# Router weights padded to 128 columns, and an accumulator cleared by ScalarE: a two-layer graph network with mixtures of experts on one Trainium2 core

## The chip, the cores and the metric

The kernel runs on one core of one Trainium2 chip. The metric is the device time of one execution in microseconds (us), taken as the median of several runs. The core has five engines that run their own instruction streams and meet only at semaphores: TensorE (PE in the profile, with its weight loads as PEld), VectorE (DVE), ScalarE (ACT), GpSimd (POOL) and SyncE (SP), which here issues most of the DMAs.

## The reference, cut to what matters

Four layers run one after the other on 6250 rows of 256 numbers and 100,000 edges sorted by destination. Everything is fp32.

```
x = x + graph_attention(layernorm(x), edges)      # 8 heads of 32
x = x + gated_ffn(layernorm(x))                   # shared MLP + 4 experts, top 2 of a softmax gate
x = x + mean_aggregate(layernorm(x), edges)       # then batch norm, relu
x = x + top1_ffn(layernorm(x))                    # 32 experts
```

The two layers that the change touches:

```
# graph attention, for every edge (s, d)
e   = leaky_relu(eh[s] + ee + et[d])
a   = exp(e - max over d) / sum over d
rst[d] = sum over the edges of d of  a * ft[s]

# gated feed-forward
gates = softmax(x @ gW + gb)          # gW is 256 x 4
top2  -> softmax of the two values -> weights of the experts' outputs
```

## The kernel before, in words

The program is a chain of stages with a barrier between them. `front` computes projected rows `ft_rows`, scores and index tables. `attend` does the softmax over edges and the weighted sums. `rank_rows` writes the sums to DRAM. `gated_experts` is the first feed-forward layer. `sum_segments`, `rank_rows`, `mean_route` and `expert_tiles` are the second half; the change does not touch them.

**attend.** The edges are laid out as 784 tiles of 128 edges, in 49 chunks of 16 tiles. For each tile GpSimd issues one indirect DMA (line 978) that gathers 128 rows of `ft_rows` into slot `c % 5` of the chunk ring `G` (`GX`, `G3`, `G4`). Four chunks are gathered already in `front` (line 511). From the sixth chunk on (`c >= GS`, number 5 counted from zero) GpSimd waits at every fourth tile until TensorE has multiplied the same tiles of the chunk that held the slot before (line 977). Per chunk, VectorE adds the scores (line 1169, `SCT`, which waits for the chunk's gathers), runs the softmax, builds one-hot matrices `AHOT` (lines 1180 and 1181) and weights the gathered rows (line 1281). TensorE multiplies rows by one-hots (line 1132). ScalarE writes the products into the accumulator `ACC` (lines 1059 and 1037), 128 partitions by 12,760 columns, at the rank of each destination. It runs two exponentials per chunk for VectorE (lines 1020 and 1024). The work on chunk 0 before its first product is `first` on each engine: VectorE's `scores`, `maxima`, `onehots`, `sums` and so on, and ScalarE's `penalties`, `exponentials`, `chain`.

`ACC` has to be zero where no edge writes. GpSimd clears it with one memset (line 961) just before its first gather of the stage, chunk 4's, and ScalarE waits for `acc_zero` before its first write (line 1042).

SyncE loads the score parts of each chunk (line 989). After the last of these it loads the feed-forward weights (line 995), the router's `GW` among them. When chunks 45, 46 and 47 have been multiplied, it reloads `x` into `GX`, piece by piece (line 1004).

**gated_experts.** The 6250 rows are 50 tiles of 125; a group is two tiles, so there are 25 groups. Written out by hand, group g on TensorE is: hidden layers of the shared MLP and the four experts (line 1906), transpose of the gate weights (line 1893, waits for VectorE's `gate_rows`), transpose of the next group's rows (line 1874), second layers (lines 1906 and 1913), spreading of the gate weights and biases (lines 1935 and 1940), then the next group's router logits (line 1885), then output layers (lines 1947 and 1952). The logits are four matmuls (2 tiles x 2 halves of the 256 features): the transposed rows `fxT` are the stationary operand, 125 columns, and `GW`, 4 columns wide, is streamed. The profile shows each fp32 matmul of this kind as two records, so eight records per group. VectorE waits for the last of them (line 1705) and then runs `gates`, a chain of small operations, later `normed` and `weigh`, which end in `gate_rows` (line 1736).

Of the kernel before, what the change touches and what calls it, by code (L numbers as in the profile page):

```python
# [22 lines left out]
ACT = mybir.ActivationFunctionType  # L23
AX = mybir.AxisListType

P = 125
N, E, D = 6250, 100000, 256
# [15 lines left out]
UT = 16  # L43
# [801 lines left out]
def attend(nc, sb, ps, sem, sems, pace, FT, PRED, CONTU, WHOLE, GX, g_in, ident, iota, SRCT, RELT, GOES, BASEI, ACC,  # L845
# [14 lines left out]
    with ExitStack() as s:  # L860
# [51 lines left out]
        sel, sel2 = sem("sel_set"), sem("sel_T")  # L912
        set_ready = sem("attend_set")
        pre_in = sems("pre_in", SL)
        pre_free, acc_zero = sem("pre_free"), sem("acc_zeroed")
        e_ready, u_ready, v_ready, x_ready = sem("scores_T"), sem("scores_U"), sem("scores_less_max"), sem("scores_exp")
        pen_ready, q_ready, qs_ready = sem("pen_ready"), sem("ends_ready"), sem("ends_by_head")
        xa_ready, xe_ready, s_ready, su_ready = sem("chain_args"), sem("chain_exp"), sem("shares_ready"), sem("shares_before")
# [14 lines left out]
        with nc.Block() as block:  # L933
            @block.gpsimd
            def _(pool):
                for one in (HSEL, HSELT):
                    nc.gpsimd.memset(one[:, :], 1.0).then_inc(sel, 1)
                nc.gpsimd.memset(FSEL[:, :, :], 1.0).then_inc(sel, 1)
                pool.wait_ge(sel, 3)
                n = 3  # L940

                for one, pat, base, mul in ((HSEL, [[-UT, H0]], 0, 1), (HSEL, [[UT, H0]], UT - 1, -1),
                                            (HSELT, [[1, 128]], 0, -UT), (HSELT, [[-1, 128]], UT - 1, UT)):
                    nc.gpsimd.affine_select(out=one[:, :], in_=one[:, :], compare_op=ALU.is_ge, fill=0.0,
                                            base=base, pattern=pat, channel_multiplier=mul).then_inc(sel, 1)
                    n += 1
                    pool.wait_ge(sel, n)

                for sign, base in ((1, 0), (-1, HD - 1)):
                    nc.gpsimd.affine_select(out=FSEL[:, :, :], in_=FSEL[:, :, :], compare_op=ALU.is_ge, fill=0.0, base=base,  # L950
                                            pattern=[[128 * sign, KD], [sign, 128]], channel_multiplier=-HD * sign).then_inc(sel, 1)
                    n += 1
                    pool.wait_ge(sel, n)

                nc.gpsimd.iota(BU[:, :], pattern=[[-1, UT]], base=0, channel_multiplier=1,
                               allow_small_or_imprecise_dtypes=True).then_inc(sel2, 1)

                for t in range(GF * UT, ES):
                    c, m = divmod(t, UT)
                    if t == GF * UT:  # L960
                        nc.gpsimd.memset(ACC[:, :], 0.0).then_inc(acc_zero, 1)
                    if t == GS * UT:
                        PADT, SEL = FFN["PADT"], FFN["SEL"]
                        nc.gpsimd.memset(PADT[:, 0:PW - 1], 0.0)
                        nc.gpsimd.memset(PADT[:, PW - 1:PW], float(SKIP)).then_inc(fw_set, 1)
                        pool.wait_ge(fw_set, 1)
                        nc.gpsimd.memset(SEL[:, :, :], 1.0).then_inc(fw_pad, 1)
                        pool.wait_ge(fw_pad, 1)

                        nc.gpsimd.affine_select(out=SEL[:, :, :], in_=SEL[:, :, :], compare_op=ALU.is_ge, fill=0.0, base=0,  # L970
                                                pattern=[[128, SEL.shape[1]], [1, 128]], channel_multiplier=-EH2).then_inc(fw_pad, 1)
                        pool.wait_ge(fw_pad, 2)
                        nc.gpsimd.affine_select(out=SEL[:, :, :], in_=SEL[:, :, :], compare_op=ALU.is_ge, fill=0.0, base=EH2 - 1,
                                                pattern=[[-128, SEL.shape[1]], [-1, 128]], channel_multiplier=EH2)
                    if m % WB == 0 and c >= GS:

                        pool.wait_ge(prod[NBK - 1], (c - GS) * CPB + m // NBK + 1)
                    pool.indirect_dma_start(G[c % GS][:, m, :], None, FT[:, :],  # L978
                                            bass.IndirectOffsetOnAxis(ap=SRCT[:, t:t + 1], axis=0)
                                            ).then_inc(g_in[c % GS], 16)  # L980

            @block.sync
            def _(sp):
# [7 lines left out]
                sp.sem_inc(pre_free, SL)  # L991
                unrolled(NCH, SL, lambda c, k, i: None, load)

                for to, of in weights:
                    sp.dma_start(to, of, allow_slow_non_contiguous=True).then_inc(fw_in, 16)
                x, X, xm_in, bias, BI, bi_in = more
# [11 lines left out]
            def _(act):  # L1008
# [13 lines left out]
                def chain(c):  # L1022
                    act.wait_ge(xa_ready, c + 1)
                    nc.scalar.activation(XA[:, :, :], XA[:, :, :], ACT.Exp).then_inc(xe_ready, 1)

                def first(c, k, i):
                    act.sem_inc(fc_ready[1], 1)
                    for step in (penalties, exponentials, chain):
                        step(c)
                    penalties(c + 1)  # L1030

                def finish(h, n):
# [5 lines left out]

                def rest(c, k, i, more):
                    steps = {3: exponentials, 9: chain}  # L1040
                    if c == 0:
                        act.wait_ge(acc_zero, 1)
                    for h in range(2):
                        act.load(regs[h], BASEI[0:1, ds(c * UT + h * HT, HT)])
                        for j in range(HT):
# [470 lines left out]
def ffn_buffers(sb, s):  # L1516

    NB = NG * EH2 // 128
    shapes = {"S1": [128, KD, SH1], "S2": [128, KD, SH2], "S3": [128, D], "E1": [128, KD, NG, EH1], "E2": [128, NG, EH2],
              "E3": [128, NB, D], "OB3": [WROW + NG + 1, D], "GW": [128, KD, NG], "GBB": [P, NG], "B1": [128, KD], "B2": [128, 1],  # L1520
              "C1": [128, NG], "C2": [128, NB], "SEL": [NG, NB, 128], "PADT": [128, PW], "BI": [P, D]}
    return {n: sb(s, f"ffn_{n}", shape) for n, shape in shapes.items()}


def ffn_weights(F, sW1, sb1, sW2, sb2, sW3, sb3, eW1, eb1, eW2, eb2, eW3, eb3, gW, gb):
# [4 lines left out]
        (F["S3"][:, :], sW3[:, :]),  # L1530
        (F["OB3"][WROW:WROW + NG, :], eb3[:, :]),
        (F["OB3"][WROW + NG:WROW + NG + 1, :], sb3.rearrange("(o n) -> o n", o=1)),
        (F["GW"][:, :, :], gW.rearrange("(k p) n -> p k n", p=128)), (F["GBB"][:, :], gb.partition_broadcast(P)),
        (F["B1"][:, :], sb1.rearrange("(k p) -> p k", p=128)), (F["B2"][:, :], sb2.rearrange("(p o) -> p o", o=1)),
        (F["C1"][:, :], eb1.rearrange("e p -> p e")),
    ]
# [12 lines left out]
def gated_experts(nc, sb, ps, sem, sems, RSUMD, RANKI, XND, F, x_in, bi_in, X, ST, MEAN, RSTD, ident, ones, epsc, SORTD):  # L1549
# [7 lines left out]
    with ExitStack() as s:  # L1557
# [49 lines left out]
        with nc.Block() as block:  # L1607
# [19 lines left out]
            def _(dve):  # L1627
# [74 lines left out]
                def gates(g):  # L1702

                    dve.wait_ge(l_ready, g + 1)
                    nc.vector.tensor_tensor(g_["l"][:, :, :], pG[0:P, 0:GT * NG].rearrange("p (k e) -> p k e", e=NG),
                                            GBB[:, :].unsqueeze(1).to_broadcast([P, GT, NG]), ALU.add).then_inc(l_read, 1)
                    dve.drain()
                    nc.vector.tensor_reduce(r_["mx"][:, :], g_["l"][:, :, :], AX.X, ALU.max)
# [152 lines left out]
            def _(pe):  # L1861
# [16 lines left out]
                def logits(g, k):  # L1878
                    pe.wait_ge(x_ready, g + 1)

                    pe.wait_ge(wt_copied, g + 1)
                    for m in range(GT):
                        o = pG[0:P, m * NG:(m + 1) * NG]
                        for c in range(KD):
                            last = nc.tensor.matmul(o, xT[k][:, c, m * P:(m + 1) * P], GW[:, c, :], start=(c == 0),
                                                    stop=(c == KD - 1))
                    last.then_inc(l_ready, 1)
# [672 lines left out]
```

## Time and profile before

| | us |
|---|---|
| median of 3 runs | 3366.17 (3363.21 to 3370.33) |
| the profiled execution's own time | 3367.67 |
| its span on the core | 3365.8 |
| attend (405 to 1372 of the span) | 967 |
| rank_rows and the start of the gated layer (1372 to 1434) | 62 |
| gated_experts from its first logits (1434 to 1872) | 438 |
| second half (1872 to the end) | 1494 |

The span is what the profiler saw between the first and the last instruction; the execution's own time is 1.9 us longer. Over the whole span TensorE is busy 74%, VectorE 57%, GpSimd 54% and ScalarE 38% of the time, but these shares mix stages with different limits. What a change is worth is read from the stage in which it lies.

### The profile page before, as it was taken

The numbers are of one execution on the slowest core, as the hardware profiler recorded it, in microseconds if no ns is written. First come the engines' busy times: TensorE is split into PE (matmuls) and PEld (weight loads), VectorE is DVE, ScalarE is ACT, GpSimd is POOL, SyncE is SP. The second block draws the span as 40 slices with busy tenths as digits, with TensorE's granted clock in tenths as the row PEclk, the third lists the DMA queues.
The fourth block names the chain that finished last, engine by engine and source line by source line (L and its number), as shares of the span: only waits on it lengthen the run. The fifth ranks groups of instructions, "written<-read, shape, count | busy, mean of one in ns | idle before, by whom it ended". The sixth has DMA issues, their size and how long they took to land. (4 is left out here: it accounts for less than half of the span.)

```text
span 3365.8 us, 49930 instructions
## 1 busy us (share of the span) xinstructions
PE 2499.3 (74%) x12770; PEld 2079.5 (62%) x12770; DVE 1930.4 (57%) x6044; ACT 1278.5 (38%) x4608; POOL 1811.0 (54%) x1886
## 2 busy tenths in 40 slices
PE   5997767666666666478878688788888888657078
PEld 5886656666665555356666566666666666546067
DVE  7971388888888887467555433333333333366245
ACT  2331145555554544432333333333333333354023
POOL 0007777777777776121000477777777777250545
PEclk9986688888878877678899656665655565755589
DMA  7345644444444446530000233333333333310443
GB/s 206 95 120 131 193 110 112 111 112 111 112 111 112 112 112 153 185 104 24 25 25 1 89 106 106 105 105 105 105 106 106 106 105 105 113 55 7 112 140 88
DMA packets 263656, 348.46 MB, mean 104 GB/s; under 512 B 153546, under 2 KB 193600, under 8 KB 262120
## 3 DMA queue, kind: packets, MB, share of 16 engines
q0 software_dynamic: 87936, 235.05, 24.9%
q1 hardware_dynamic: 175446, 110.32, 12.8%
q8 instruction: 104, 1.70, 0.2%
q14 instruction: 170, 1.38, 0.1%
HBM read 288.25 MB, written 61.20 MB: 104 GB/s over the span
## 5 line engine op out<-in xcount | busy, mean ns | idle before, releaser
L1379 POOL DMA_INDIRECT Gb<-normed_rows,SRCT x784 | 743.3, 948 | 566.4 <-SPq L1371 327.7
L1400 PE MATMUL pAb<-HOTb,Gb 128*128 128x128 f32 x3136 | 839.9, 424 | 155.3 <-DMA Gb<-normed_rows,SRCT 125.8
L1400 PEld LDWEIGHTS pAb<-HOTb,Gb 128*128 128x128 f32 x3136 | 658.1, 296 | 337.5 <-DMA Gb<-normed_rows,SRCT 279.6
L1440 DVE TENSOR_TENSOR ACC<-ACC,pAb 128x256 f32 x784 | 330.6, 422 | 644.1 <-PE pAb L1400 571.4
L978 POOL DMA_INDIRECT GX<-ft_rows,SRCT x432 | 414.2, 959 | 131.5 <-issue 130.3
L1059 ACT ACTIVATE ACC<-apA 128x254 f32 x784 | 301.0, 384 | 424.1 <-PE apA L1132 349.6
L1132 PE MATMUL apA<-AHOT,GX 128*128 128x129 f32 x1920 | 306.9, 330 | 84.7 <-DVE GX L1281 84.5
L1132 PEld LDWEIGHTS apA<-AHOT,GX 128*128 128x128 f32 x1920 | 292.1, 242 | 103.1 <-DVE GX L1281 102.6
L1419 ACT ACTIVATE HOTb<-OFFb 128x1024 f32<-128x1024 f32 x98 | 103.6, 1057 | 606.5 <-PE pAb L1400 606.4
L978 POOL DMA_INDIRECT G<-ft_rows,SRCT x288 | 275.5, 957 | 87.6 <-issue 86.0
L1415 ACT ACTIVATE OFFb<-iota,NRELb 128x128 f32<-128x128 f32 x784 | 239.6, 388 | 7.5 <-issue 1.0
L1132 PE MATMUL apA<-AHOT,G 128*128 128x129 f32 x1216 | 190.9, 326 | 53.8 <-DVE G L1281 51.5
L1132 PEld LDWEIGHTS apA<-AHOT,G 128*128 128x128 f32 x1216 | 181.2, 238 | 65.9 <-DVE G L1281 62.8
L1601 POOL DMA_INDIRECT Y<-sums_by_rank,RANKI x50 | 48.5, 970 | 179.3 <-DVE GX L1648 85.4
L1281 DVE TENSOR_TENSOR GX<-GX,apV 128x1024 f32<-128x1024 f32 x120 | 143.1, 1192 | 0.0
L533 PEld LDWEIGHTS pS<-VB,eT 128*128 128x128 f32 x784 | 116.6, 236 | 33.3 <-ACT eT L624 31.4
L1060 ACT ACTIVATE FL<-apA 128x4 f32<-128x4 f32 x784 | 134.5, 172 | 0.0
L533 PE MATMUL pS<-VB,eT 128*128 128x16 f32 x784 | 120.9, 299 | 16.9 <-ACT eT L624 12.3
L497 POOL DMA_INDIRECT C<-et_rows,DXI x1 | 2.3, 2272 | 234.9 <-DMA et_rows<-ETS 234.9
L2166 POOL DMA_INDIRECT rows_by_expert<-PAY,POSI x50 | 49.7, 995 | 140.3 <-DVE POSI L2357 125.3
L1181 DVE TENSOR_TENSOR AHOT<-apL,RELT 128x1024 f32<-128x1024 f32 x98 | 122.5, 1250 | 0.0
L2418 POOL DMA_INDIRECT out_dram<-sO,sID x80 | 77.9, 973 | 74.9 <-issue 42.0
(381 smaller groups left out, 4453.7 us busy)
## 6 DMA issues: line engine op xcount, KB each, us to landing
ebuf<-in_edge_attr_dram SPq DMA_DIRECT2D x49, 448.0 KB
Gb<-normed_rows,SRCT POOLq DMA_INDIRECT x784, 2.8
rows_by_expert<-ffn_PADT SPq DMA_DIRECT2D x1, 10360.0 KB
sT<-rows_by_expert SPq DMA_DIRECT2D x80, 129.5 KB, 2.2
GX<-ft_rows,SRCT POOLq DMA_INDIRECT x480
sums_by_rank<-rrowa SPq DMA_DIRECT2D x49, 128.0 KB, 1.7
sums_by_rank<-rrowb SPq DMA_DIRECT2D x49, 128.0 KB, 1.7
GX<-in_x_dram SPq DMA_DIRECT2D x11, 560.0 KB
```

The source lines that it names most:

```text
L533: last = nc.tensor.matmul(pS[:, m * 2 * H0:(m + 1) * 2 * H0], eT[c % 2][:, m * EP:(m + 1) * EP], VB[:, :], start=True, stop=True)
L978: pool.indirect_dma_start(G[c % GS][:, m, :], None, FT[:, :], bass.IndirectOffsetOnAxis(ap=SRCT[:, t:t + 1], axis=0)).then_inc(g_in[c % GS ...
L1059: nc.scalar.activation(acc[:, :, ds(r + 1, EP - 1)], sums[:, :, 1:EP], ACT.Copy)
L1060: nc.scalar.activation(FL[:, :, f:n + 1:n - f], sums[:, :, 0:HW:EP], ACT.Copy).then_inc(pfree[b], 1)
L1132: last = nc.tensor.matmul(pA[b][:, f * HW:(f + 1) * HW], G[c % GS][:, m, f * 128:(f + 1) * 128], HOT[c % 2][:, m, :], start=True, stop=True)
L1181: nc.vector.tensor_tensor(HOT[c % 2][:, h * HT:(h + 1) * HT, 0:EP], pL[0:EP, 256:256 + EP].unsqueeze(1).to_broadcast([EP, HT, EP]), RELT[: ...
L1281: nc.vector.tensor_tensor(v, v, pV[0:EP, 0:128].rearrange("p (h m) -> p h m", m=UT)[:, :, m:m + WB].rearrange("p h m -> p m h").unsqueeze( ...
L1379: pool.indirect_dma_start(G[g % R][m][:, :], None, TABLE[:, :], bass.IndirectOffsetOnAxis(ap=SRCT[:, t:t + 1], axis=0)).then_inc(g_in[g % ...
L1400: last = nc.tensor.matmul(pA[b][:, o:o + EP], G[k][m][:, c * 128:(c + 1) * 128], HOT[k % 2][:, m, :], start=True, stop=True)
L1415: nc.scalar.activation(OFF[k2][:, m, :], iota[0:EP, 0:EP], ACT.Abs, bias=NREL[k2][:, m:m + 1])
L1419: nc.scalar.activation(HOT[k2][:, :, :], OFF[k2][:, :, :], ACT.Relu, bias=1.0, scale=-1.0).then_inc(hot[k2], 1)
L1440: last = nc.vector.tensor_tensor(acc[:, :, ds(b, EP)], acc[:, :, ds(b, EP)], pA[q][:, o:o + KD * EP].rearrange("p (c r) -> p c r", c=KD), ...
```

## The change

1. GpSimd no longer clears `ACC`. The semaphore `acc_zero` and ScalarE's wait for it are gone. ScalarE clears `ACC` itself, in two halves of 6,380 columns: an activation Copy of a broadcast constant column with scale 0. The first half stands between `penalties(0)` and `exponentials(0)`, the second between `exponentials(0)` and `chain(0)`.
2. The router's weight tile `GW` grows from 4 to 128 columns per half (1 KB per partition). GpSimd zeroes it before chunk 5's gathers, and SyncE waits for that before it loads the weights; the load fills columns 0 to 3.
3. The four logit matmuls of a group stream 128 columns in place of 4. They write 256 columns of the bank in place of 8, and VectorE reads 4 of each 128.

```diff
@@ attend, GpSimd
                 for t in range(GF * UT, ES):
                     c, m = divmod(t, UT)
-                    if t == GF * UT:
-                        nc.gpsimd.memset(ACC[:, :], 0.0).then_inc(acc_zero, 1)
                     if t == GS * UT:
-                        PADT, SEL = FFN["PADT"], FFN["SEL"]
+                        PADT, SEL, GW = FFN["PADT"], FFN["SEL"], FFN["GW"]
+                        nc.gpsimd.memset(GW[:, :, :], 0.0).then_inc(fw_set, 1)
                         nc.gpsimd.memset(PADT[:, 0:PW - 1], 0.0)
                         nc.gpsimd.memset(PADT[:, PW - 1:PW], float(SKIP)).then_inc(fw_set, 1)
-                        pool.wait_ge(fw_set, 1)
+                        pool.wait_ge(fw_set, 2)
@@ attend, SyncE
                 unrolled(NCH, SL, lambda c, k, i: None, load)
+                sp.wait_ge(fw_set, 2)
                 for to, of in weights:
@@ attend, ScalarE
+                def clear(h):
+                    half = KD * NR // 2
+                    nc.scalar.activation(ACC[:, h * half:(h + 1) * half], iota[:, 0:1].to_broadcast([128, half]), ACT.Copy,
+                                         scale=0.0)
+
                 def first(c, k, i):
                     act.sem_inc(fc_ready[1], 1)
-                    for step in (penalties, exponentials, chain):
-                        step(c)
+                    penalties(c)
+                    clear(0)
+                    exponentials(c)
+                    clear(1)
+                    chain(c)
                     penalties(c + 1)
@@
                 def rest(c, k, i, more):
                     steps = {3: exponentials, 9: chain}
-                    if c == 0:
-                        act.wait_ge(acc_zero, 1)
@@ ffn_buffers, ffn_weights
-"GW": [128, KD, NG]
+"GW": [128, KD, 128]
-        (F["GW"][:, :, :], gW.rearrange("(k p) n -> p k n", p=128)), (F["GBB"][:, :], gb.partition_broadcast(P)),
+        (F["GW"][:, :, 0:NG], gW.rearrange("(k p) n -> p k n", p=128)), (F["GBB"][:, :], gb.partition_broadcast(P)),
@@ gated_experts, VectorE
-                    nc.vector.tensor_tensor(g_["l"][:, :, :], pG[0:P, 0:GT * NG].rearrange("p (k e) -> p k e", e=NG),
+                    nc.vector.tensor_tensor(g_["l"][:, :, :], pG[0:P, 0:GT * 128].rearrange("p (k e) -> p k e", e=128)[:, :, 0:NG],
@@ gated_experts, TensorE
-                        o = pG[0:P, m * NG:(m + 1) * NG]
+                        o = pG[0:P, m * 128:(m + 1) * 128]
                         for c in range(KD):
                             last = nc.tensor.matmul(o, xT[k][:, c, m * P:(m + 1) * P], GW[:, c, :], start=(c == 0),
                                                     stop=(c == KD - 1))
```

## Rows read from the trace of the kernel before

**Rows 1.** Busy time by stage: stretch, its length, each engine's busy us, clock, DMA.
```profile
core 0: us, PE busy (x) PEld busy (x) DVE busy (x) ACT busy (x) POOL busy (x), PEclk, DMA share, GB/s
405.00:1372.00 967.00, 637.06 (x3822) 573.42 (x3822) 814.46 (x2816) 489.84 (x2549) 704.28 (x736) 0.81 0.47 114
...
1434.00:1872.00 438.00, 353.85 (x1736) 277.09 (x1737) 264.70 (x1237) 142.16 (x317) 34.27 (x35) 0.87 0.12 36
```

**Rows 2.** Instruction groups of GpSimd in attend: busy us, mean ns, idle before.
```profile
L978 POOL DMA_INDIRECT GX<-ft_rows,SRCT x432 | 414.2, 959 | 131.5 <-issue 130.3 <-PE apA L1132 1.2
...
L961 POOL MEMSET ACC<- 128x12760 f32 x1 | 10.7, 10732 | 0.0
...
L964 POOL MEMSET ffn_PADT<- 128x258 f32 x1 | 0.3, 333 | 0.0
```

**Rows 3.** Timeline of VectorE: start us, us; the score step of chunks 1, 29, 46, 47.
```profile
427.31 0.37 DVE L1169 TENSOR_TENSOR SCT<-GX,PRE 128x128 f32<-128x128 f32 x1
...
948.80 0.36 DVE L1169 TENSOR_TENSOR SCT<-G,PRE 128x128 f32<-128x128 f32 x1
...
1290.74 0.37 DVE L1169 TENSOR_TENSOR SCT<-GX,PRE 128x128 f32<-128x128 f32 x1 [2.08 <-DMA GX<-ft_rows,SRCT]
...
1318.75 0.37 DVE L1169 TENSOR_TENSOR SCT<-GX,PRE 128x128 f32<-128x128 f32 x1 [9.54 <-DMA GX<-ft_rows,SRCT]
```

**Rows 4.** Timeline of the stage's start, ScalarE and GpSimd.
```profile
406.56 1.28 ACT L1020 ACT_TABLE_LOAD   x1
...
407.90 10.73 POOL L961 MEMSET ACC<- 128x12760 f32 x1
...
422.51 0.24 ACT L1024 ACTIVATE XA<-XA 8x48 f32<-8x48 f32 x1 [8.85 <-DVE XA L1235]
...
433.64 0.38 ACT L1059 ACTIVATE ACC<-apA 128x254 f32 x1 [0.15 <-issue]
...
440.50 0.95 POOL L978 DMA_INDIRECT GX<-ft_rows,SRCT  x1 [0.16 <-issue]
```

**Rows 5.** VectorE's copy into the one-hots: ns min/median/max, first and last start.
```profile
L1180 DVE COPY AHOT<-GOES x49: 169/175/5093, 413.6 to 1342.2; 128x16 f32<-128x16 f32 x49
```

**Rows 6.** Instruction groups of ScalarE, kept apart by shape.
```profile
L1419 ACT ACTIVATE HOTb<-OFFb 128x1024 f32<-128x1024 f32 x98 | 103.6, 1057 | 606.5 <-PE pAb L1400 606.4
...
L1014 ACT ACTIVATE CTU<-CONTU 128x129 f32<-128x129 bf16 x49 | 15.3, 312 | 11.1 <-DVEq L1153 5.6
```

**Rows 7.** Timeline of SyncE's queue near the end of attend: the first reloads of x.
```profile
1306.42 1.63 SPq L1004 DMA_DIRECT2D GX<-in_x_dram  x4
```

**Rows 8.** Waits in 1434 to 1872: us in total, times, longest.
```profile
DVE gate_l L1705 <- PE fpG L1885: 12.9, 25, 3.7
```

**Rows 9.** Timeline of gated_experts: VectorE's first gate step in four groups, logits of the last.
```profile
1647.43 0.17 DVE L1705 TENSOR_TENSOR gate_l<-fpG,ffn_GBB 125x8 f32<-125x8 f32 x1 [0.32 <-PE fpG L1885]
...
1661.78 0.17 DVE L1705 TENSOR_TENSOR gate_l<-fpG,ffn_GBB 125x8 f32<-125x8 f32 x1 [0.31 <-PE fpG L1885]
...
1802.58 0.17 DVE L1705 TENSOR_TENSOR gate_l<-fpG,ffn_GBB 125x8 f32<-125x8 f32 x1 [0.31 <-PE fpG L1885]
...
1815.50 1.03 PE L1885 MATMUL fpG<-ffn_GW,fxT 128*125 128x4 f32 x8
...
1816.58 0.17 DVE L1705 TENSOR_TENSOR gate_l<-fpG,ffn_GBB 125x8 f32<-125x8 f32 x1 [0.31 <-PE fpG L1885]
```

**Rows 10.** TensorE records: one's ns min/median/max, then two merged runs of records.
```profile
L1885 PE MATMUL fpG<-ffn_GW,fxT x200: 250/250/373, 1433.4 to 1850.7; 128*125 128x4 f32 x100
...
478.24 2.05 PE L1132 MATMUL apA<-AHOT,GX 128*128 128x129 f32 x16 [1.13 <-DVE GX L1281]
...
1653.30 3.54 PE L1906 MATMUL fpM<-fxT,ffn_E 128*128 128x250 f32 x16
```

**Rows 11.** TensorE's busy time and granted clock (third number; 1.00 is 2.4 GHz).
```profile
1644.10:1647.50 3.40, 3.40 (x27) 1.00 0.00 0
1647.50:1650.90 3.40, 3.40 (x9) 0.51 0.02 5
```

More of the change, by code:

```diff
@@ L914, in attend @@
         pre_in = sems("pre_in", SL)
-        pre_free, acc_zero = sem("pre_free"), sem("acc_zeroed")
+        pre_free = sem("pre_free")
         e_ready, u_ready, v_ready, x_ready = sem("scores_T"), sem("scores_U"), sem("scores_less_max"), sem("scores_exp")
@@ L1519, in ffn_buffers @@
     shapes = {"S1": [128, KD, SH1], "S2": [128, KD, SH2], "S3": [128, D], "E1": [128, KD, NG, EH1], "E2": [128, NG, EH2],
-              "E3": [128, NB, D], "OB3": [WROW + NG + 1, D], "GW": [128, KD, NG], "GBB": [P, NG], "B1": [128, KD], "B2": [128, 1],
+              "E3": [128, NB, D], "OB3": [WROW + NG + 1, D], "GW": [128, KD, 128], "GBB": [P, NG], "B1": [128, KD], "B2": [128, 1],
               "C1": [128, NG], "C2": [128, NB], "SEL": [NG, NB, 128], "PADT": [128, PW], "BI": [P, D]}
```

## The prediction

> **What bounds the kernel now.** I read the busy time by stage first. In attend no engine is full: VectorE is busy 814 of 967 us and GpSimd 704 [rows 1]. So the next view is what each of the two waits for. GpSimd's gathers cost 0.96 us each and have 0.3 us of issue time in front (131.5 us over 432), 1.25 us together; of their idle time only 1.2 us was spent waiting for a free slot [rows 2], and the 288 gathers of the other slots look the same. GpSimd runs flat out through the stage. Sixteen gathers make 20.1 us per chunk.
>
> The timeline of VectorE's score step shows who is late. From chunk 1 to chunk 29 it starts every (948.80 - 427.31)/28 = 18.6 us and waits for nothing. By chunk 46 it waits 2.08 us for gathered rows [rows 3]; all of the 17 chunks from 30 to 46 wait so and come about 20.1 us apart. VectorE uses up the lead of four chunks, and after chunk 29 the gather stream alone sets the time. A microsecond taken from GpSimd before its last gather is a microsecond off the stage, provided VectorE and the slots allow it.
>
> In the gated layer TensorE is busy 354 of 438 us [rows 1], but it is not alone on the path. VectorE's first gate step waits for the logits in all 25 groups [rows 8], and the loop logits, gates, gate weights, transposes, second layers, logits closes: 14.00 us from one gate step to the next, whose logits started 1.08 us before it [rows 9]. What is added to the end of the logits is added to each group.
>
> **The change part by part.**
>
> *The memset.* It held GpSimd 10.73 us from 407.90, directly ahead of chunk 4's gathers [rows 2, 4]. They start that much earlier: -10.7 us. `GW` is zeroed in the same stream, 256 columns; the memset of 258 columns took 0.33 us [rows 2]: +0.3. SyncE's new wait is for that memset, done at about 430; the weight loads behind it come after the last score-part load, hundreds of microseconds later, and are as many as before: nothing.
>
> *VectorE in the prologue.* One of the 49 copies of line 1180 took 5.09 us against a median of 0.175, the one at 413.6 that ran beside the memset; it ended with it [rows 4, 5]. Two steps behind it were stretched as well. Without the memset chunk 0's chain moves up by about 3.5 us: 4.9 for the copy, less 1.3 of one-hot and scan work that ran meanwhile. The Trainium skill, "SBUF — State Buffer", section "Who interferes with whom", says that VectorE and GpSimd share a port pair as an exclusive lock, so the later one blocks fully, and that ScalarE has ports of its own. The trace agrees with the first half (5.09 us). The page would have the new clearing disturb nobody; no row shows it.
>
> *ScalarE's clearing.* 1024 columns take 1.057 us and 129 take 0.312, so 0.83 ns per column and 0.2 fixed [rows 6]; a half of 6,380 columns takes 5.5 us. If all of it went at 1.057/1024 it would be 6.6. Chunk 0: the table load at 406.56 [rows 4] marks the end of the penalties; first half to 412.1, table load of 1.28 to 413.3. The first exponential feeds the work behind the copy of 413.6 [rows 5], so it is about on time. Second half 413.7 to 419.2; the next exponential, at 422.51 before [rows 4], would be wanted 3.5 earlier, at 419.0. It comes 0.2 late, and VectorE has the second half of the one-hots to do in between. So the clearing hides behind VectorE's prologue. With 6.6 us halves VectorE is 0.9 us late; cover gone entirely, each half would cost up to 6.6. ScalarE's own order puts the clearing ahead of the products, the fourth of which reached it at 433.64 [rows 4].
>
> *The slot wait.* Chunk 5's first gather was at 440.50; now it wants to go at 440.5 - 10.7 + 0.3 = 430.1. It needs four tiles of chunk 0 multiplied, which was so just before 433.6 [rows 4] and, 3.5 earlier, at 430.0. So this wait goes from nothing to 0 to 0.6 us; I take 0.2. If VectorE gained nothing it would be 3.4. After that TensorE moves at 18.6 per chunk and GpSimd at 20.1, so the slots open up. Does VectorE still fall behind the gathers before the end? It starts 10.2 - 3.5 = 6.7 us behind the shifted stream and gains 1.5 per chunk: five chunks later than 30. Chunk 35 is well before 48. Attend: -10.7 + 0.3 + 0.2 = -10.2; bounds -10.6 and -7.0.
>
> *The end of attend.* The reload of x starts when chunk 45 is multiplied, at 1306.4, and chunk 47's rows come 9.54 us late beside it [rows 3, 7]. Both sides of that collision move with the gathers, so it stays as it is.
>
> *The logits.* Before, eight records in 1.03 us, one of them 0.25 [rows 9, 10]: (1.03 - 0.25)/7 = 0.111 us apart, though only 4 columns are streamed. So the weight load of 125 columns sets the pace. Streaming 250 columns, 16 records take 3.54: about 0.21 apart, so 128 columns need 0.108, which fits under 0.111. The run with 129 columns and 128 weights has 16 in 2.05, about 0.118 apart [rows 10]. The pace is hardly changed; what is added is the tail of the last record, between nothing (its bound by the load) and 124 of 250 columns of 0.21, 0.10. Per group: low 0.02, high 7 x 0.007 + 0.10 = 0.15. I take 0.08, times 24 loops: +1.9 us; bounds 0.5 and 3.6. VectorE's strided read is of 8 elements still: nothing. The Trainium skill, "TensorE: Matmul & The Clock Gate", section "Back-to-back issue gap", speaks against the widening: a warm matmul of 64 columns or fewer takes about 60 cycles and one of 128 takes 134. Those 74 cycles at 2.4 GHz are 31 ns; times 8 and 24 it is an estimate of 5.9 us and would make the sum -5.3. The pace of 0.111 at 4 columns says that the floor here is the load, so I do not follow it.
>
> *The clock.* At 1647.5 the granted clock fell from 2.4 to 1.2 GHz for 3.4 us although TensorE had been busy for all of the 3.4 us before [rows 11]. That stretch held the half-width second layers, the 4- and 5-row spreads and the 4-column logits: busy by the profile, but with a small part of the array. Five of the stage's falls are of that kind; the others follow idle time. Wider logits may prevent those five. It buys little: with such a fall the loop took 1661.78 - 1647.43 = 14.35 us, without one 14.00 [rows 9], because TensorE waits for VectorE anyway. At most 5 x 0.35 = 1.8 us, at least 0; I take -1.
>
> **Sum.** -10.2 + 1.9 - 1.0 = -9.3. The profiled execution (3367.67) would take 3358.4; it lies 1.5 above the median, so the median goes from 3366.2 to about **3357**. By the bounds: -10.6 + 0.5 - 1.8 = -11.9 and -7.0 + 3.6 = -3.4, so 3354 to 3363. The runs shown spread over 7 us, so 0.2% (6.7 us) is about what a measurement of this kernel can tell from no change, and the forecast lies just beyond it.
>
> **Rivals.**
>
> *The clearing delays chunk 0.* If ScalarE's halves take well over 6.6 us, or a table load comes in front of each, VectorE starts late, and chunk 5's gather stalls at its slot. From 0.1 us of lost shift on, each microsecond costs one. With 3.4 lost: 3360 to 3361. For it: the wait is tight. Against: ScalarE idled 8.85 us ahead of the second exponential [rows 4]. Chance 0.12.
>
> *The memset was hidden.* Then attend does not move and the logits cost 1 to 2: 3367. For it: VectorE, not GpSimd, paces the first 29 chunks. Against: 18 chunks at the end wait for rows. Chance 0.10.
>
> *The clock does more.* Wide logits also bring the full clock back sooner after idle stretches, and the longer loops shrink. If the five falls and two later rises each gave 3.4 us of full clock back [rows 11] and half of that showed, it would be 7 x 1.7 = 12 at the very most; the gate chain leaves perhaps -3 to -7 of it, 3350 to 3354. Against: the gate chain on VectorE binds. Chance 0.13.
>
> *The other side: stream no longer hides the load.* If at 128 columns load and stream add up (0.111 + 0.108 per record), a group is longer by 8 x 0.108 = 0.86 us, 24 groups by 20.7: 3366.2 - 10.2 + 20.7 = 3377. It decides from 0.43 us per group on. Against: 0.118 at 129 columns. Chance 0.04.
>
> Forecast as summed, 3352 to 3361: 0.61. Of the forecast's chance about a sixth lies on the near side of 0.2%. Faster by over 0.2%: 0.50 + 0.13 + 0.03 = 0.66. Within 0.2%: 0.11 + 0.10 + 0.09 = 0.30. Slower: 0.04. The range that holds 8 in 10 takes in the nearer half of the clock rival and the first rival: 3351 to 3364.
>
> **What would show it.** Chunk 4's first gather at about 408, chunk 5's at 430 with at most 0.6 us of wait on TensorE; two ScalarE activations of 5.5 us; line 1180's maximum below 1 us; score steps waiting for rows from about chunk 35, chunk 46's at 1280.5; the logits' eight records in 1.05 to 1.2 us; fewer clock falls behind them. I am wrong if the slot wait is longer, if the score step of chunk 46 moves by less than 9 us, or if the gated layer changes by more than 4 us either way.

## The result, and the profile after

| | before | after |
|---|---|---|
| median (20 runs each, one chip) | 3364.44 us (3362.14 to 3370.33) | 3370.98 us (3364.72 to 3378.85) |
| ratio to before, 95% interval | | 1.0017 (1.0010 to 1.0023), about +5.7 us |
| profiled execution: own time, span | 3367.67, 3365.8 | 3368.51, 3365.8 |

The forecast was 3357 us, 0.27% under the median that it started from; the kernel is 0.17% slower. That is still inside the 0.2% within which a measurement tells little, but on the other side of no change, and outside the range of 3351 to 3364 us. The two profiled executions have the same span, so between them something was won and lost again. The traces show where.

The attention stage won what was forecast, and some 2 us more. Timeline of the changed kernel at the stage's start, with ScalarE first, then GpSimd (these answer to [rows 2, 4]); the stage itself starts 1.2 us later than before here, at 406.24 for 405.06:

```profile
407.62 5.50 ACT L1029 ACTIVATE ACC<-iota 128x6380 f32<-128x6380 f32 x1
413.13 1.28 ACT L1020 ACT_TABLE_LOAD   x1
414.79 5.50 ACT L1029 ACTIVATE ACC<-iota 128x6380 f32<-128x6380 f32 x1
420.20 0.23 ACT L1024 ACTIVATE XA<-XA 8x48 f32<-8x48 f32 x1
...
409.28 0.97 POOL L977 DMA_INDIRECT G<-ft_rows,SRCT  x1
...
429.04 0.34 POOL L962 MEMSET ffn_GW<- 128x256 f32 x1
...
431.49 0.95 POOL L977 DMA_INDIRECT GX<-ft_rows,SRCT  x1 [0.54 <-PE apA L1139]
```

Two halves of 5.50 us, the second exponential 2.3 us earlier than in [rows 4], and a slot wait of 0.54 us where it was 0.16 of issue time. The copy into the one-hots has lost its outlier (view of one line: ns min/median/max), and the score steps of chunks 1, 33, 34, 46 and 47 show where VectorE falls behind the gathers (timeline of VectorE), then the reload of x:

```profile
L1187 DVE COPY AHOT<-GOES x49: 153/175/425, 414.8 to 1329.1; 128x16 f32<-128x16 f32 x49
```

```profile
424.95 0.37 DVE L1176 TENSOR_TENSOR SCT<-GX,PRE 128x128 f32<-128x128 f32 x1
...
1018.28 0.37 DVE L1176 TENSOR_TENSOR SCT<-G,PRE 128x128 f32<-128x128 f32 x1
1037.44 0.37 DVE L1176 TENSOR_TENSOR SCT<-G,PRE 128x128 f32<-128x128 f32 x1 [0.81 <-DMA G<-ft_rows,SRCT]
...
1279.39 0.37 DVE L1176 TENSOR_TENSOR SCT<-GX,PRE 128x128 f32<-128x128 f32 x1 [2.04 <-DMA GX<-ft_rows,SRCT]
1306.64 0.37 DVE L1176 TENSOR_TENSOR SCT<-GX,PRE 128x128 f32<-128x128 f32 x1 [8.81 <-DMA GX<-ft_rows,SRCT]
...
1295.09 1.72 SPq L1004 DMA_DIRECT2D GX<-in_x_dram  x4
```

Chunk 46 comes 1290.74 - 1279.39 = 11.35 us earlier than in [rows 3], and the first gate step of the gated layer stands at 1422.89 for 1435.28, 12.4 us earlier. With the later start of the stage the move at chunk 46 is 12.5 us, where -10.2 was summed. The 720 gathers were busy 687.3 us in this execution and 689.7 in the one before, which is about the difference.

The gated layer then gives all of it back: from its first gate step to its last it takes 1851.50 - 1422.89 = 428.6 us, and took 415.7. Gate steps in four groups, as in [rows 9], and the logits' records:

```profile
1641.29 0.17 DVE L1712 TENSOR_TENSOR gate_l<-fpG,ffn_GBB 125x8 f32<-125x8 f32 x1 [0.42 <-PE fpG L1892]
1657.35 0.17 DVE L1712 TENSOR_TENSOR gate_l<-fpG,ffn_GBB 125x8 f32<-125x8 f32 x1 [0.42 <-PE fpG L1892]
1671.44 0.17 DVE L1712 TENSOR_TENSOR gate_l<-fpG,ffn_GBB 125x8 f32<-125x8 f32 x1 [0.42 <-PE fpG L1892]
1687.44 0.17 DVE L1712 TENSOR_TENSOR gate_l<-fpG,ffn_GBB 125x8 f32<-125x8 f32 x1 [0.41 <-PE fpG L1892]
```

The four steps bound three loops. The one of 14.09 us was 14.00 before, the 0.10 us of the wider logits. But the other two are 16.06 and 16.00 us. Before, the eleven short loops of the layer took 13.99 to 14.36 us, and none took 16. TensorE's timeline inside the first of them shows the place:

```profile
1640.12 1.14 PE L1892 MATMUL fpG<-ffn_GW,fxT 128*125 128x128 f32 x8
...
1650.86 0.43 PE L1900 MATMUL fpG<-ident,gate_rows 125*128 125x125 f32 x2 [1.94 <-DVE gate_rows L1743]
1651.12 0.91 PE L1881 MATMUL fpT<-ident,fxn 125*128 125x125 f32 x4
1651.82 1.88 PE L1913 MATMUL fpM<-h,ffn_S 128*128 128x250 f32 x4
1653.63 1.55 PE L1920 MATMUL fpM<-e,ffn_E 128*64 128x250 f32 x8
```

and the windows view (third number from the end: granted clock) says at which clock:

```profile
1645.00:1648.40 3.40, 3.40 (x18) 3.05 (x17) 2.25 (x15) 2.00 (x6) 0.00 (x0) 1.00 0.01 2
1651.30:1654.70 3.40, 3.40 (x14) 2.25 (x14) 0.41 (x1) 1.06 (x2) 0.00 (x0) 0.51 0.00 0
```

TensorE idles 1.94 us for the gate weights, and just behind that the clock falls to 1.2 GHz. The second layers of the shared MLP take 1.88 us and took 1.01 in the same position of undisturbed loops. This is the stretch between gate weights and next logits, which is on the loop's path. Before, five falls of 3.4 us started right behind the logits [rows 11], where TensorE has time to spare; the changed kernel has none there. What such a fall costs is less than the prediction read from [rows 9]. These are, from the kernel before, the gate weights' transposes in the loop of the fall at 1647.5, then two gate steps and the loop between them, in which the clock did not fall:

```profile
1657.01 0.43 PE L1893 MATMUL fpG<-ident,gate_rows 125*128 125x125 f32 x2 [0.17 <-DVE gate_rows L1736]
...
1675.77 0.17 DVE L1705 TENSOR_TENSOR gate_l<-fpG,ffn_GBB 125x8 f32<-125x8 f32 x1 [0.31 <-PE fpG L1885]
...
1690.10 0.17 DVE L1705 TENSOR_TENSOR gate_l<-fpG,ffn_GBB 125x8 f32<-125x8 f32 x1 [0.31 <-PE fpG L1885]
...
1675.77:1690.10 14.33, 12.49 (x71) 10.02 (x71) 7.94 (x41) 5.18 (x12) 0.00 (x0) 1.00 0.00 1
```

The short loops alternate between 14.00 and 14.35 us by themselves, and the loop with the fall, 14.35 us, is no longer than this one at full clock, 14.33. The fall used up TensorE's idle time ahead of the gate weights, 0.17 us left of some 1.85, and cost nothing. The other short loop with such a fall took 14.31 where its turn would give 14.00. So such a fall costs 0 to 0.3 us.

The 12.9 us come apart as follows. Four of the changed kernel's short loops have the fall in the costly place, four times some 1.6 us = 6.4. The logits' own part is 24 x 0.10 = 2.4. The remaining 4 are in the slower loops, which vary from one kernel to the next. Two of them took 17.02 us before and 18.65 and 21.25 after, but the same two take 18.54 and 21.01 in e1b below, which has the narrow router and wins as much back in two others. So these 4 us are not shown to be the router's.

### The profile page after: what moved, and what is told of

It is laid out like the page before. It is cut to its first block and busy times, and to the rows that moved or that the text cites. A ratio compares the mean times of both kernels' runs of the same rounds, so it can differ in the third digit from the quotient of the medians.

```text
span 3365.8 us, 49932 instructions
## 1 busy us (share of the span) xinstructions
PE 2483.2 (74%) x12770; PEld 2066.6 (61%) x12770; DVE 1926.3 (57%) x6044; ACT 1288.8 (38%) x4610; POOL 1794.8 (53%) x1886
```

## The experiments

Two numbers are read off each trace beside the ratio. One is the gated layer's length from the first gate step to the last. The other is TensorE's gap ahead of the gate weights' transposes in the short loops, which alternate between a shorter and a longer one. "Behind" and "ahead" are in the order of TensorE's program. Layer, gap and loops come from one profiled execution of each kernel, the ratio from all its executions (5 to 20). The ratios are to the kernel before on the same chip, with 95% intervals.

| kernel | router's columns | ratio | gated layer, us | gap, us | loops of 16 us |
|---|---|---|---|---|---|
| before (its profile) | 4 | 1 | 415.7 | 1.50 / 1.85 | 0 |
| after | 128 | 1.0017 (1.0010 to 1.0023) | 428.6 | 1.60 / 1.94 | 4 |
| e1b, clearing only | 4 | 0.9966 (0.9955 to 0.9978) | 416.3 | 1.51 / 1.86 | 0 |
| e2b, wide router only | 128 | 1.0041 (1.0028 to 1.0055) | 428.6 | 1.62 / 1.95 | 4, and 1 of 17.5 |
| e3b, filler behind the logits | 4 | 0.9965 (0.9953 to 0.9977) | 417.5 | 0.65 / 0.98 | 0 |
| e4b, one matmul ahead of the logits | 4 | 0.9969 (0.9959 to 0.9979) | 419.4 | 1.52 / 1.86 | 0 |
| e8, VectorE 0.07 later | 4 | 0.9986 (0.9978 to 0.9995) | 422.3 | 1.57 / 1.91 | 2 |
| e9, VectorE 0.24 later | 4 | 1.0023 (1.0014 to 1.0032) | 436.9 | 1.74 / 2.09 | 3, and 2 of 17.5 |
| e7, wide, filler in the gap | 128 | 0.9996 (0.9987 to 1.0005) | 424.0 | 0.72 / 1.05 | 0 |
| e10, 64 columns | 64 | 1.0017 (1.0006 to 1.0027) | 423.8 | 1.56 / 1.90 | 4 |
| e17, wide, VectorE 0.16 earlier | 128 | 0.9962 (0.9948 to 0.9977) | 415.6 | 1.44 / 1.79 | 0 |
| e18, wide, VectorE 0.32 earlier | 128 | 0.9966 (0.9954 to 0.9978) | 412.6 | 1.28 / 1.63 | 0 |
| e19, clearing only, VectorE 0.32 earlier | 4 | 0.9949 (0.9935 to 0.9963) | 409.1 | 1.17 / 1.52 | 0 |

**The two halves of the change.** e1b takes the router's part back (main lines):

```diff
-"GW": [128, KD, 128]
+"GW": [128, KD, NG]
-                        nc.gpsimd.memset(GW[:, :, :], 0.0).then_inc(fw_set, 1)
-                sp.wait_ge(fw_set, 2)
-                        o = pG[0:P, m * 128:(m + 1) * 128]
+                        o = pG[0:P, m * NG:(m + 1) * NG]
```

> The change without its wide router: the weights stay 4 columns wide, the accumulator is cleared by ScalarE. Both theories: the attention stage keeps its gain of 10 to 12 us and the gated layer runs as before (a loop of 14.00 us, the slower ones 14.3), so 3351 to 3355 us, ratio 0.9960 to 0.9972. Rival (the loss comes from the earlier start of the gated layer, or from anything else in the clearing, not from the columns): the gated layer loses 10 us or more here too, with loops of 16 us, ratio 0.999 to 1.002.

e2b is the kernel before with the router's part alone.

> The kernel before with the wide router alone (GpSimd clears the accumulator). If the columns make the loss by themselves: loops of 14.10 with several of 16 us, 13 to 19 us lost in the gated layer, ratio 1.004 to 1.0055. Rival (the columns cost only their own time, 0.1 us a loop): 2.4 us, ratio 1.0007.

Clearing alone gives 0.34% (11 us) and leaves the gated layer as it was; the wide router alone costs 0.41% (14 us). Its short loops of 16.07, 16.03, 16.06 and 16.08 us stand where the changed kernel has its four, and it has one more of 17.47, with a longer fall in the same place. So the loss is the router's, it does not need the earlier start, and it is over five times the 2.4 us that the longer logits add.

**Why the router costs that: columns, lateness, or the gap.** e3b puts idle work behind the logits, e4b puts a narrow matmul ahead of them:

```diff
@@ e3b, behind the logits' semaphore
+                    for m in range(GT):
+                        for c in range(KD):
+                            nc.tensor.matmul(pT[0:P, 0:128], xT[k][:, c, m * P:(m + 1) * P], S1[:, c, 0:128], start=True, stop=True)
@@ e4b, ahead of the logits
+                    nc.tensor.matmul(pG[0:P, 64:64 + NG], xT[k][:, 0, 0:P], GW[:, 0, :], start=True, stop=True)
```

> Clearing by ScalarE and the narrow router, and four matmuls of 128 columns into a bank that nobody reads behind the logits' semaphore: TensorE is as busy behind the logits as with the wide router, and VectorE gets the logits as early as before. Theory A (what hurts is that the logits end later, so that TensorE's gap ahead of the gates' weights grows and the half clock falls into the stretch after it): no loops of 16 us, 0.995 to 0.997. Theory B (what hurts is the work itself, which takes the half clock away from the harmless place behind the logits and leaves it to the harmful one behind the gates' weights): 1.000 to 1.001 with loops of 16 us.

> Clearing by ScalarE, the narrow router, and one more matmul of 4 columns ahead of the logits, so that they end some 0.1 us later and stay narrow. Theory A (lateness): loops of 16 us, ratio 1.001 to 1.004. Theory B (columns): 14.1 us a loop and none of 16 us, ratio 0.998.

e3b ended as theory A has it. Four matmuls of 128 columns behind the logits bring no loop of 16 us (two of 15.2 are the dearest of the short ones), so streaming wide columns there does not do it. It is a weaker test than it was meant to be: theory B needs the falls behind the logits to be taken away, and e3b still has four of them, two of which start the loops of 15.2. e7 and e17 below test that part. But e4b went against theory A as it was put: the short loops are about 14.2 and 14.55 us, and none has 16. The timeline of e4b says why: the gap is still 1.85.

```profile
1646.16 0.43 PE L1899 MATMUL fpG<-ident,gate_rows 125*128 125x125 f32 x2 [1.85 <-DVE gate_rows L1741]
...
1649.85 0.38 PE L1887 MATMUL fpG<-ffn_GW,fxT 128*125 128x4 f32 x2
1650.09 1.01 PE L1891 MATMUL fpG<-ffn_GW,fxT 128*125 128x4 f32 x8
```

A matmul ahead of the logits makes VectorE and TensorE's own following work late alike, so nothing opens between them. Its ratio carries a reserve: of its twelve executions eight lie at 3353.4 to 3356.3 us, the profiled one among them, and four at 3361.5 to 3367.9, and whether these have loops of 16 us isn't known. The theory had to be sharpened: not the lateness of the logits, but that VectorE is late against TensorE. The wide logits do that, because what follows them on TensorE closes up. The logits end 0.10 us later, but the second of the two output layers starts 1.83 us after the logits' start in the changed kernel (1640.12, 1641.95) and 1.84 in e1b (1666.44, 1668.28).

**The gap alone.** e8 and e9 hold VectorE back and touch nothing on TensorE:

```diff
@@ e8, in gates
+                    nc.vector.tensor_tensor(r_["f"][:, :], GBB[:, 0:GT], GBB[:, 0:GT], ALU.add)
                     nc.vector.tensor_reduce(r_["mx"][:, :], g_["l"][:, :, :], AX.X, ALU.max)
@@ e9, in gates
                     nc.vector.tensor_reduce(r_["mx"][:, :], g_["l"][:, :, :], AX.X, ALU.max)
+                    dve.drain()
+                    nc.vector.tensor_reduce(r_["mx"][:, :], g_["l"][:, :, :], AX.X, ALU.max)
```

> Clearing by ScalarE, the narrow router, and one small VectorE operation more between reading the logits and their maximum (some 0.08 us), so that VectorE is later and TensorE is not: the gap ahead of the gates' weights grows from 1.50 and 1.85 us to about 1.6 and 1.93, as with the wide router, without a column of work. The gap theory: loops of 16 us as in the changed kernel, ratio 0.999 to 1.002. The column theory: only the 0.08 us of each loop, no loop of 16 us, ratio 0.997 to 0.998.

> As the run before it with a drained operation instead (the maximum taken twice, 0.24 us later): gaps of about 1.74 and 2.09 us. The gap theory: at least as many loops of 16 us, ratio 1.001 to 1.006. The column theory: 0.24 us a loop, 5.8 us in all, no loop of 16 us, ratio 0.998 to 0.9985.

With 4 columns, e8 has two loops of 16.03 and 16.05 us. One of them on TensorE:

```profile
1646.82 0.49 PE L1899 MATMUL fpG<-ident,gate_rows 125*128 125x125 f32 x2 [1.91 <-DVE gate_rows L1742]
1647.11 1.04 PE L1880 MATMUL fpT<-ident,fxn 125*128 125x125 f32 x4
1647.94 1.88 PE L1912 MATMUL fpM<-h,ffn_S 128*128 128x250 f32 x4
```

The same 1.88 us as in the changed kernel, with no wide column in the program. e8's ratio lies between the two forecasts (half the falls), e9's is where only the gap theory put it: 20.6 us more in the gated layer than e1b, of which 24 x 0.24 = 5.8 is VectorE's own. (The profiled execution of e9 lies almost 6 us above its median, so the 20.6 is rather high.) Columns are not needed for the loss.

**The gap closed, columns kept.** e7 fills it with idle matmuls, e10 halves the columns (main line):

```diff
@@ e7, ahead of weights(g)
+                    for f in range(4):
+                        nc.tensor.matmul(pG[:, 128:256], S1[:, 0, 0:128], xT[k][:, 0, 0:128], start=True, stop=True)
@@ e10
-"GW": [128, KD, 128]
+"GW": [128, KD, 64]
```

> The changed kernel with its wide router, and four matmuls of 128 columns that nobody reads ahead of the wait for the gates' weights, so that TensorE idles some 0.5 to 0.9 us less there. The gap theory: no loop of 16 us, ratio 0.997 to 0.9985 (the wide router's own 2.4 us stay). The column theory (the wide logits themselves move the half clock): loops of 16 us as in the changed kernel, ratio 1.000 to 1.003.

> The changed kernel with the router's weights widened to 64 columns instead of 128. If a weight load, not the columns, sets a logits matmul's time at this width, they end as early as with 4 columns. The gap theory: gaps stay at 1.50 and 1.85 us, no loop of 16 us, ratio 0.996 to 0.998. The column theory: half the columns bring back at least some loops of 16 us, ratio 0.999 to 1.002.

e7 has no loop of 16 us, with all 128 columns, and no fall behind the logits either, which speaks against theory B. Its loops are as long as the undisturbed ones of the changed kernel (14.10 and 14.43 us), so the loop's length by itself does not bring the falls. It gains less than forecast, because the filler itself costs: e5, the narrow router with the same four matmuls, has a gated layer of 422.0 us, and e15 (the same kernel again) 421.1, against 416.3 and 415.7 with clearing alone. 416.3 + 5.7 + 2.4 for the logits makes 424.4, and e7 took 424.0.

e10 did not separate the theories, as its premise was false: at 64 columns the logits already end later than at 4 (records of 279 ns on average for 253) and the gap opens by 0.05 us. It has four loops of 16 us, at a gap of 1.88 in this one:

```profile
1650.55 0.43 PE L1900 MATMUL fpG<-ident,gate_rows 125*128 125x125 f32 x2 [1.88 <-DVE gate_rows L1743]
1655.88 1.08 PE L1892 MATMUL fpG<-ffn_GW,fxT 128*125 128x64 f32 x8
```

So half the padding has the whole loss: the ratio is the changed kernel's.

**VectorE earlier.** The strongest form takes time out of VectorE's chain and leaves the wide router alone. In `first_max` the first product is by ones; a copy gives the same values, and the next operation need not wait for it:

```diff
@@ first_max, in the loop over e
+                        if e == 0:
+                            nc.vector.tensor_copy(mark[:, :, 0], g_["eq"][:, :, 0])
+                            nc.vector.tensor_tensor(r_["t"][:, :], r_["t"][:, :], g_["eq"][:, :, 0], ALU.subtract)
+                            dve.drain()
+                            continue
```

It is 0.16 us a call. e17 has it in the second call alone, e11, e13 and e18 (one kernel, three chips) in both, with the wide router; e12, e14 and e19 are the same with the narrow one.

> The changed kernel, wide router and all, with a shorter chain on VectorE: in first_max the first of the four products (by ones) becomes a copy that the next operation needn't wait for, some 0.16 us less in each of two calls, the same values. The gap ahead of the gates' weights shrinks from 1.60 and 1.94 us to about 1.28 and 1.62 with TensorE's work unchanged. The gap theory: loops of 13.8 and 14.1 us and none of 16, 5 to 8 us for the shorter chain and about 8 for the falls, ratio 0.9955 to 0.9980. The column theory: slower loops of 15.7 us stay, only the shorter chain counts, ratio 0.9992 to 1.001.

> The same shorter chain with ScalarE's clearing and the narrow router, the version meant to beat both. If VectorE's chain sets the loop here, 24 loops of up to 0.32 us: 5 to 8 us under the run with clearing alone, ratio 0.9943 to 0.9955. If TensorE's clock gives it back: no better than that run, 0.996 to 0.998.

> Clearing by ScalarE, the narrow router and the four idle matmuls ahead of the wait for the gates' weights: what the filler costs by itself, to read the wide router with filler (0.9996) rightly. If the filler is paid only in the loops that TensorE paces: 2 to 5 us over clearing alone, ratio 0.997 to 0.9985, so that the wide router keeps a loss of its own of some 3 to 8 us beside it. If the filler is hidden everywhere: 0.9966, and the wide router's loss with filled gaps is 10 us and not explained by the gap.

These three ran on a chip on which the kernel before takes 3865 us. Ratios: e11 0.9978 (0.9963 to 0.9993), e12 0.9983 (0.9971 to 0.9995), e5 0.9991 (0.9979 to 1.0003). The short loops came as forecast for the gap theory: 13.75 and 14.11 us with the wide router, none of 15.7. The next chip was of the same kind (3870 us):

> The changed kernel with the shorter chain on VectorE, on another chip. Gap theory: gated layer's loops 13.75 and 14.11 us and none of 16; with the attention stage's gain of 10 to 12 us, ratio 0.9955 to 0.9975. If the wide router loses in another way too: 0.998 or more.

> Clearing alone with the shorter chain, on another chip: loops of 13.66 and 14.01 us, 5 us under clearing alone, ratio 0.9945 to 0.9960. If TensorE's clock gives it back: as clearing alone, 0.9966.

> Clearing alone with four idle matmuls ahead of the wait for the gates' weights, on another chip: 2 to 6 us over clearing alone, paid in the slower loops that TensorE paces, ratio 0.997 to 0.9985. If hidden: 0.9966.

> Clearing alone, the common base on this chip: 0.9955 to 0.9978, as measured. If chips differ in this too: outside.

e13 0.9973 (0.9960 to 0.9986), e14 0.9984 (0.9973 to 0.9996), e15 0.9993 (0.9982 to 1.0005), e16 1.0001 (0.9990 to 1.0012). Clearing alone, worth 0.34% on the first chip, is worth nothing on this one. The groups of GpSimd in e16's attention stage show that the condition of [rows 2] is gone:

```profile
L976 POOL DMA_INDIRECT GX<-ft_rows,SRCT x432 | 411.5, 953 | 246.1 <-issue 109.0 <-PE apA L1137 79.9 <-remote 57.2
```

A gather costs the same 953 ns, but GpSimd waits 79.9 us for free slots in this group, where [rows 2] had 1.2. None of VectorE's 49 score steps waits for gathered rows there; they come (1667.62 - 528.20)/48 = 23.7 us apart, where the gathers need 20.1. So the gathers no longer set the pace, and a microsecond of GpSimd is covered. What does set it, and why these two chips run that stage slower, was not found (ScalarE's largest wait, 353.6 us, ends with nothing the profile names).

The last three, on a chip with 3372 us for the kernel before:

> The changed kernel with the shorter first step in the second of the two calls of first_max alone, 0.16 us: gaps of about 1.44 and 1.78 us, the narrow router's or a little less, with the wide router's columns. Gap theory: loops of 13.93 and 14.28 us and none of 16, so at least as good as the narrow router: 0.9955 to 0.9975 where the attention stage has its gain. Column theory: loops of 15.9 us, 0.9995 to 1.0015. On a chip where clearing alone moves nothing: 0.9985 to 1.0005 against 1.003.

> The wide router with 0.32 us less on VectorE: gap theory 0.9945 to 0.9965 where the attention stage has its gain (0.9973 and 0.9978 where it has none, measured).

> The narrow router with 0.32 us less on VectorE: 0.9940 to 0.9960 where the attention stage has its gain (0.9983 and 0.9984 where it has none, measured). If wide and narrow differ by less than their intervals, the wide router costs nothing beyond the loops of 16 us.

e17 is the answer in one kernel. Gates and logits in its timeline:

```profile
1633.83 0.17 DVE L1717 TENSOR_TENSOR gate_l<-fpG,ffn_GBB 125x8 f32<-125x8 f32 x1 [0.42 <-PE fpG L1897]
1648.11 0.17 DVE L1717 TENSOR_TENSOR gate_l<-fpG,ffn_GBB 125x8 f32<-125x8 f32 x1 [0.42 <-PE fpG L1897]
```

```profile
1643.24 0.43 PE L1905 MATMUL fpG<-ident,gate_rows 125*128 125x125 f32 x2 [1.79 <-DVE gate_rows L1748]
...
1646.93 1.14 PE L1897 MATMUL fpG<-ffn_GW,fxT 128*125 128x128 f32 x8
```

The logits are as wide and as long as in the changed kernel (1.14 us), the gap is 1.79, the loop between the two gate steps is 14.28, and the ratio is 0.9962: 0.16 us less on VectorE per group, 3.8 us in all if nothing else moved, took 18 us off the changed kernel's place (1.0017, measured apart from it). e19 is the best kernel of the study, 0.9949, faster than both. On this chip the narrow router leads the wide one (0.9949 for 0.9966, the intervals overlap), on the other two the wide one is level or ahead (0.9978 for 0.9983, 0.9973 for 0.9984). What the wide router costs without its loops of 16 us is thus too small for these runs; the trace has 0.10 us a loop.

## Why the prediction was wrong

*The memset, the prologue, ScalarE's clearing, the slot wait, the end of attend: right.* Chunk 4's gathers start 9.5 us earlier on the clock of the trace, 10.7 with the later start of the stage; two activations of 5.50 us, as estimated; the stall of line 1180 gone (425 ns at most); 0.54 us of slot wait inside the 0 to 0.6; score steps wait from chunk 34, forecast about 35; chunk 46 at 1279.4, forecast 1280.5. The second exponential, which the prediction wanted 3.5 us earlier, came 2.3 earlier on the clock of the trace and 3.5 in the stage. e1b is the measurement: 3356.7 us, ratio 0.9966, -11.5 us where -10.2 was summed. The Trainium skill, "SBUF — State Buffer", section "Who interferes with whom", gave ScalarE its own ports; the trace now agrees, since the copy beside the clearing took 0.15 us at 414.79. The Trainium skill, "ScalarE: Activation LUTs", section "What ACT_TABLE_LOAD costs", has 186 ns and 0.833 ns a column for such an activation, which makes 5.50 us for 6,380 columns, an estimate; the trace has 5.50.

*The logits: the size right, the place half right.* Eight records in 1.14 us, 0.10 us a loop, 2.4 us; forecast 0.08 and 1.9. The estimate of 5.9 us that the prediction did not follow is too high for this case, and the rival in which stream and load add up is out. The pace is unchanged, 0.109 us from one record to the next at 4, 64 and 128 columns. But the tail of the last record, on which the prediction put all the rest, is longer by only 0.023 us. The larger part, 0.08, is between the first record and the second: 0.13 us at 4 columns (1632.36 to 1632.49 in the kernel before), 0.21 at 128 (1640.12 to 1640.33).

*The clock: this step failed, and with it the sign.* The prediction took -1, "at most 5 x 0.35 = 1.8 us, at least 0", on the ground that TensorE waits for VectorE anyway. Two things are wrong in it. The 0.35 us was a misreading: it compares a loop that has a fall with one that has none, but the loops alternate between these two lengths at full clock too (14.33 at 1675.77), so there was little to win: of the five falls one cost nothing and one 0.3 us, and the other three stand in loops of 16.7 to 17.0 us. And the step let the change only remove falls. It did remove them: every profile with 64 or 128 columns has no fall that starts behind the logits, and every one with 4 columns has 2 to 11. But others came behind the gate weights, on the path, at some 1.6 us each. The range of the term should have reached to one such fall in every second loop. In place of -1 the gated layer lost some 10 us beside the logits' own in the profiled execution (12.9 less 2.4), of which 6.4 are the four falls. By the ratios it is more, 5.7 + 11.5 - 2.4 = 14.8 us; the 5.7 and the 11.5 come from two measurements.

*What made it fall there* was told apart by the experiments. Wide columns are neither needed (e8, e9) nor enough (e7, e17, e18 and e3b's filler). Holding VectorE back against TensorE by 0.07 to 0.24 us brings the falls, and letting it catch up by 0.16 takes them away. e7 and e4b keep the gap closed or as it was in loops of 14.1 to 14.6 us, and have none. Each short loop of 16 us had a longer gap than any of the kernel before, 1.88 to 2.09 us against 1.86 at most. But there is no sharp limit between: e1b passes a gap of 1.90 us with a loop of 14.39, and the changed kernel one of 1.98 with 14.47. Which of the long gaps is hit differs from loop to loop and was not settled. The Trainium skill, "TensorE: Matmul & The Clock Gate", section "HAM oscillation — how this bites in real kernels", describes the same thing in a coarser form: a loop that waits once per pass, 3 to 5 us for a DMA there, finds its clock halved at the start of every pass. The traces agree that the half clock comes behind such a wait. They differ in size: waits of 1.88 to 2.09 us are enough here, and only some passes are hit.

*The rival "the clock does more"* looked at the right engine and had the wrong sign; no rival had the clock working against the change. "The memset was hidden" was a statement about one chip: true where e16 ran (1.0001), false where e1b ran (0.9966). The other slow chip had no kernel with the clearing alone.

## What to carry to other kernels

When an edit delays one engine of a two-engine loop, ask what it does to the other's idle gap, and where a fall of TensorE's clock would land if it came there; price it at the half clock on the path, with either sign, also when no fall stands there now. Before a difference between two loops is put down to a fall of the clock, look for a loop of the longer kind without one. A tenth of a microsecond that costs 2.4 us by itself can cost 14, and 0.16 us taken off the right chain can give 18 back.

An edit that frees an engine pays only where that engine sets the pace, and this can differ between chips that run the same program: look at the idle time in front of its instructions on more than one.

Two independent edits in one change should be timed apart: here -0.34% and +0.41% looked like nothing.

## What the runs showed of the hardware

- A clear of 6,380 fp32 columns by a ScalarE activation takes 5.50 us; beside it a VectorE copy took 0.15 us and a gather of GpSimd 0.95, as elsewhere. GpSimd's memset of 12,760 took 10.73 us and stalled a VectorE copy for 5.09.
- Widening the streamed side of an fp32 matmul with a 125-column weight load from 4 to 64 columns lengthens eight records from 1.03 to 1.08 us, to 128 columns to 1.14. The pace between records stays at 0.109 us; the step from the first to the second grows from 0.13 to 0.16 and 0.21. The second output layer behind them starts no later (1.83 us after the logits' start for 1.84), so the receiving engine is later against TensorE.
- The granted clock fell to 1.2 GHz for 3.4 us right behind the 4-column logits 2 to 11 times in every profiled gated layer with the narrow router, and never behind those of 64 or 128 columns. With the gap of 1.88 us or more ahead of the gate weights it can fall behind these instead, which lengthens a loop from 14.35 to some 16 us.
- Two of the experiments' five chips run the attention stage so much slower that the kernel before takes 3865 and 3870 us for 3364 to 3372, with gathers of unchanged length (953 ns) and the gated layer unchanged (415.7 us in e16, 416.3 in e1b).
